# Adding x1 into the residual rows by an accumulating DMA instead of by identity products on TensorE

## The reference

```
x  = x + block(layernorm(x))                     # sublayer 1
     block(y): h  = layernorm(y, gamma, beta)
               h  = spiral_conv(h)               # long complex convolution over the 1024 tokens
               x1 = h + y
               return silu(layernorm(x1) @ w1 + b1) @ w2 + b2 + x1      # 128 -> 512 -> 128
x  = x + moe(layernorm(x))                       # sublayer 2
     moe(y):   the 2 best of 8 experts by y @ router, softmax over the two;
               each expert gelu(y @ w1[e] + b1[e]) @ w2[e] + b2[e]      # 128 -> 256 -> 128
```

## Time and profile before

| | us |
|---|---|
| three timed runs | 463.04, 464.27, 464.46 |
| their median | 464.27 |
| span of the profiled execution | 462.5 |
| TensorE busy in the span | 379.4 |
| VectorE busy | 357.4 |
| ScalarE busy | 321.8 |
| GpSimd busy | 268.1 |

### The profile page before, as it was taken

One profiled execution on the slowest core, in us unless ns is written; L12 is line 12 of the kernel. 1 busy time (PEld: TensorE's weight loads), 2 busy tenths in 40 slices (PEclk: granted clock), 3 DMA queues, 4 the chain that ended last, 5 costly groups with the idle time before them and its releaser, 6 DMA issues.

```text
span 462.5 us, 11382 instructions
## 1 busy us (share of the span) xinstructions
PE 379.4 (82%) x2812; PEld 339.3 (73%) x2812; DVE 357.4 (77%) x1329; ACT 321.8 (70%) x773; POOL 268.1 (58%) x331
## 2 busy tenths in 40 slices
PE   1274189989888889988897388999999999999980
PEld 1232168678676869686876388999999999999980
DVE  7999999978999999998176238777777777767770
ACT  4873387978887888867473536777777777777740
POOL 6980827452888888485627704676555555555551
PEclk9996569989999999999999569999999999999995
DMA  7649100000020202011203232444333333333200
GB/s 254 176 143 324 48 1 1 1 1 2 0 98 1 74 26 74 26 60 38 96 2 108 86 97 86 134 143 128 108 100 95 100 103 104 108 107 104 76 4 0
DMA packets 33283, 37.42 MB, mean 81 GB/s; under 512 B 5254, under 2 KB 29331, under 8 KB 33092
## 3 DMA queue, kind: packets, MB, share of 16 engines
q1 hardware_dynamic: 27236, 23.56, 18.0%
q0 software_dynamic: 5984, 13.13, 8.2%
HBM read 19.52 MB, written 18.92 MB: 83 GB/s over the span
## 4 chain that ended last, share of the span: by engine, by line
PE 56%; DVE 16%; ACT 9%; issue 5%; POOL 4%; POOLq 0%; DVEq 0%; ACTq 0%
PE up_p L999 12%; PE turn_p L999 6%; PE down_p L1018 6%; PE route_p L1018 6%; PE up_p L1018 5%; PE down_p L835 5%; PE turn_p L807 4%; DVE stats L1098 3%; ACT rows L655 3%; PE route_p L873 3%; ACT work L628 3%; PE down_p L1008 2%; DVE work L1162 2%; PE up_p L819 2%; DVE work L1160 1%
## 5 line engine op out<-in xcount | busy, mean ns | idle before, releaser
L590 POOL DMA_INDIRECT out<-result,out_id x91 | 89.2, 980 | 89.5 <-DVE result L1484 63.8
L556 POOL DMA_INDIRECT sorted_rows<-rows,pos x64 | 77.0, 1203 | 35.7 <-DVE pos L1217 18.4
L999 PE MATMUL up_p<-xt,work 128*128 128x128 f32 x488 | 66.5, 280 | 0.0
L781 ACT ACTIVATE work<-mw_c 128x256 f32 x182 | 65.5, 414 | 0.3 <-issue 0.2
L835 PEld LDWEIGHTS down_p<-w_sb,work 128*128 128x128 f32 x512 | 60.3, 192 | 4.9 <-issue 4.8
L835 PE MATMUL down_p<-w_sb,work 128*128 128x128 f32 x512 | 63.1, 277 | 0.0
L999 PEld LDWEIGHTS up_p<-xt,work 128*128 128x128 f32 x488 | 61.0, 196 | 0.2
L766 ACT ACTIVATE hid_t<-up_p 128x512 f32<-128x512 f32 x61 | 36.4, 597 | 30.3 <-PE up_p L999 29.7
L807 PE MATMUL turn_p<-ident,work 128*128 128x128 f32 x192 | 28.6, 298 | 28.4 <-ACT work L641 10.9
L615 ACT ACTIVATE work<-up_p,b_all 128x512 f32<-128x512 f32 x64 | 41.5, 680 | 14.3 <-PE up_p L821 14.2
L807 PEld LDWEIGHTS turn_p<-ident,work 128*128 128x128 f32 x192 | 24.0, 154 | 34.4 <-ACT work L641 11.6
(11 more groups left out here) (244 smaller groups left out, 896.5 us busy)
## 6 DMA issues: line engine op xcount, KB each, us to landing
tin<-sorted_rows SPq DMA_DIRECT2D x91, 136.0 KB, 2.1
resid<-in_x SPq DMA_DIRECT2D x8, 512.0 KB, 3.8
sorted_rows<-zeros SPq DMA_DIRECT2D x29, 136.0 KB, 2.3
out<-result,out_id POOLq DMA_INDIRECT x91, 2.2
work<-in_mw SPq DMA_DIRECT2D x1, 1024.0 KB, 6.2
sorted_rows<-rows,pos POOLq DMA_INDIRECT x64, 2.5
work<-in_w SPq DMA_DIRECT2D x1, 256.0 KB
w_sb<-in_w SPq DMA_DIRECT2D x1, 256.0 KB
```

The lines of the kernel that those rows point to most:

```text
L556: g.indirect_dma_start(sorted_dram, bass.IndirectOffsetOnAxis(pos[b % 2][:, j:j + 1], 0), rows[b % ROWBUFS][:, j, :], None).then_inc(s_sor ...
L590: g.indirect_dma_start(out_rows, bass.IndirectOffsetOnAxis(out_id[k][:, :], 0), result[k][:, :], None, bounds_check=TOKENS - 1, oob_is_err ...
L781: last = s_.activation(ring[s % RING][:, k * EF:(k + 1) * EF], mw1_c[:, bass.ds(at[k], EF)], ACT.Copy)
L999: last = t.matmul(mid_p[s % DEEP][:, c * TILE:(c + 1) * TILE], ring[s % RING][:, c * 128:(c + 1) * 128], xt[s % DEEP][:, :], start=True, s ...
```

## The change

The two identity products of `mlp_down(b, 0)` are removed, for each of the eight batches. In their place GpSimd issues one DMA per batch, `add_x1(b)`, which reads `x1[b % 2]` and adds it into the batch's rows of `resid`, both in SBUF, 128 partitions of 4096 bytes (512 KB). It is issued once `x1_sum(b)` is done and the last readers of the plain x rows of the batch (the two norms on ScalarE) are through. `x2_sum(b)` gets one more wait, on that DMA's own semaphore, before it reads `resid`.

```diff
--- before.py
+++ after.py
@@ -298,6 +298,7 @@
         s_up = sem("up_done")
         s_silu = sem("silu_done")
         s_dn = sem("down_done")
+        s_res = [sem(f"x1_in_residual{b}") for b in range(BATCHES)]
         s_x2 = sem("x2_ready")
 
         s_x2m = sem("x2_moments")
@@ -538,6 +539,13 @@
                 then(g.tensor_tensor(scale1[:, :], tmp[:, 1, :], neg_half[:, 0:TPB], ALU.pow))
                 g.tensor_tensor(shift1[:, :], tmp[:, 0, :], scale1[:, :], ALU.mult).then_inc(s_sc1, 1)
 
+            def add_x1(b):
+
+                pool.wait_ge(s_x1, b + 1)
+                pool.wait_ge(s_hn, b + 1)
+                pool.wait_ge(s_xn, b + 1)
+                g.dma_start(batch_of(resid, b), x1[b % 2], accum_op=ALU.add).then_inc(s_res[b], 16)
+
             def x2_scales(b):
                 pool.wait_ge(s_x2m, b + 1)
                 after(pool, s_xm, b)
@@ -563,6 +571,8 @@
                     x1_scales(b1)
                 if live(b0):
                     x2_scales(b0)
+                if live(b1):
+                    add_x1(b1)
                 if live(b3):
                     x0_scales(b3)
                 if live(chosen_b):
@@ -574,6 +584,7 @@
             sort_constants()
             x1_scales(0)
             x0_scales(2)
+            add_x1(0)
             for i in range(LAST):
                 iteration(i)
 
@@ -827,9 +838,6 @@
                     for h in range(2):
                         t.matmul(half(down_p, h), ones[:, :], b2_hi_lo[:, :], start=True, stop=False,
                                  skip_group_check=True)
-                    for h in range(2):
-                        t.matmul(half(down_p, h), ident[:, :], x1[b % 2][:, h * TPB // 2:(h + 1) * TPB // 2, :],
-                                 start=False, stop=False, skip_group_check=True)
                 pe.wait_ge(s_silu, b * 2 * FC + 2 * c + 2)
                 for j in range(TPB):
                     last = t.matmul(down_p[:, j * D:(j + 1) * D], silu[c % 2][:, j * TILE:(j + 1) * TILE],
@@ -1110,6 +1118,7 @@
 
             def x2_sum(b):
                 v.wait_ge(s_dn, (b + 1) * FC)
+                v.wait_ge(s_res[b], 16)
                 if live(b - ROWBUFS):
                     v.wait_ge(s_sort[b - ROWBUFS], 16 * TPB)
                 d.tensor_tensor(x2_of(b), tiled(down_p[:, :]), batch_of(resid, b), ALU.add).then_inc(s_x2, 1)
```

## The result

The changed kernel takes **466.04 us** (median of 7 runs, 465.79 to 467.58) against 464.41 us of the kernel before on the same chip (7 runs): a ratio of 1.0038, 95% interval 1.0021 to 1.0055, 1.6 us more. Two later measurements gave 1.0051 (1.0032 to 1.0071) and 1.0045 (1.0029 to 1.0061).

What follows compares the result with a forecast made beforehand. It took VectorE to bound iterations 2 and 3 and a VectorE-GpSimd-ScalarE-TensorE loop iterations 4 to 6. Span 462.5 - 0.5 + 2.4 + 0.2 + 0.3 = 464.9 us, given as median 466.6 us, range 462.9 to 472.0.

Steps and rivals of the forecast that it cites:

- So 1.26 us is covered: GpSimd: each DMA issue costs 1.26 us, hidden in waits of 1.8 us in iteration 2, 5.75 in iteration 5.
- Rival 2: GpSimd becomes the bound: issue exceeds the 1.8 us of room in iterations 2 to 4; 468.3 us at 3.3 us; chance 0.12.
- The rule of the Trainium skill that I weighed: GpSimd: VectorE blocks it only in two-port modes, so writing DMA descriptors should not suffer; issue 1.26 us anywhere.
- What the wider gaps do to TensorE's clock: TensorE: waits before place grow to 2.6 to 3.6 us, clock falls to half; 2.4 + 0.2 + 0.3 us, bounds 0 to 9.2.
- 0.8 us into each of iterations 4 to 6: TensorE: the part of a clock fall left on the path there, 0.8 us three times, 2.4 us.
- the case that I had bounded by 2.1 us: TensorE in iterations 4 to 6: a low-clock stretch lasting twice as long leaves 2.1 us on the path.
- covered by the same ScalarE norm, and its gain ends there: First batch: removing its identity product gains nothing, because ScalarE's norm covers it.
- Iteration 1, given 0.3 us: TensorE in iteration 1: the low-clock stretch already there may last longer, costing 0.3 us.
- Together the gain is 0.5 us of 15.3: TensorE: of 15.3 us of removed products only 0.4 us in iteration 1 and 0.1 in the tail shorten the path.
- TensorE's busy time lower by 15 us, unless the clock is low for longer: Sign on the changed profile: no identity product, TensorE busy some 15 us less unless its clock stays low longer.
- No wait of `x2_sum` on the DMA: VectorE's x2_sum: transfer of 7.6 us, at most 15, fits at least 23 us of room; the wait costs nothing.
- Iterations 2 and 3 keep VectorE's 25.4 us: Sign on the changed profile: these iterations, bound by VectorE, should keep their 25.4 us.

Runs made afterwards that it cites:

- experiment on iteration 4 alone: Changed kernel with identity products kept and the DMA moved behind x0_scales in iteration 4 only, in front elsewhere; 464.88 us, 0.9993.
- With GpSimd in time: Changed kernel with the DMA moved behind x0_scales: products gone 466.5 us, 1.0046; identity products put back 464.1 us, 0.9996.
- filler: Changed kernel plus four products of the identity with zeros in front of place in iterations 2 to 6; 468.11 us, 1.0085, and again 467.89 us, 1.0067.
- kernel with filler in iteration 0 as well: Changed kernel, DMA behind x0_scales, zero products before place in iterations 2 to 6 and in iteration 0; 463.85 us, 0.9976; without those in iteration 0, 1.0018.
- third session's profile: Profile of the unaltered changed kernel, run again beside the repeated filler run; 466.7 us, 1.0045.
- only the DMA: Changed kernel with its identity products put back, DMA in its first place, so x1 enters the sum twice; 466.86 us, 1.0061.

## Why the prediction was right, and where it was right by luck

The time (466.6 predicted, 466.04 measured), the direction and the range held. That the number is so close is luck: one cost was left out, and the cost that was counted was put too high in the iterations for which it was worked out. The steps:

**"So 1.26 us is covered"** is the step that failed. The price of an issue was right (0.99 us and 0.3), the room was not. I read the room in iteration 2 (1.8 us) and in iteration 5 (5.75 us) and took the iterations between for one or the other. The binding place is iteration 4, the last with `x0_scales`: before, the scatters waited 0.79 us there for `pos` and `x1_scales` 0.87 us for VectorE, 1.66 us together, and the push was more than the 1.26 us, because the small instructions behind the DMA slid under VectorE's products. In iteration 2 of the changed kernel the same rows took 0.2 to 0.5 us, and 1.55 us of waiting were left. Rival 2, at 0.12, therefore came true in a mild form, in one iteration and not three, 1.7 us late where I had priced 1.5. The experiment on iteration 4 alone shows it. The DMA with the products kept costs 1.0061, 2.8 us, a term that my sum puts at nothing.

The rule of the Trainium skill that I weighed (SBUF — State Buffer, Who interferes with whom) held for what I applied it to: the DMA's issue took 1.00 us beside a scan. The 3.01 us that I set against it was the row of an indirect DMA. My summary of the section was too short. The same section also says that a VectorE instruction with two inputs in SBUF contends with a GpSimd instruction that reads SBUF. The trace agrees (1.49 us beside 0.21 for the same instruction), and it is that sentence which applied to the instructions behind the DMA.

**"What the wider gaps do to TensorE's clock"**: the mechanism was right. The waits before `place` were 2.3 to 2.6 us and 3.4 us in iteration 6 (predicted 2.6 to 2.8 and 3.6), and falls followed some of them, not all. The size is open between 0.9 and 2.3 us, and the division was wrong. With GpSimd in time, products gone against products kept is 1.0046 against 0.9996, 0.5% or 2.3 us, where the forecast was 2.9 - 0.5 = 2.4 us. But with no DMA at all the products gone cost 1.0019 (1.0000 to 1.0038), 0.9 us, and that interval leaves 2.4 us out.

I had put 0.8 us into each of iterations 4 to 6. Where the clock fell behind `place` and the low stretch was as long as the recorded one, it cost 0 to 0.3 us (read where GpSimd was in time), so the waits behind covered nearly all of it. Only where it lasted twice as long, the case that I had bounded by 2.1 us, did it cost 1.0 to 1.6 us: in iteration 6 in four profiles, in iteration 4 in one.

I also gave iteration 0 nothing, "covered by the same ScalarE norm, and its gain ends there": I had asked only whether it could gain. In three of the nine profiles without product or filler there the clock was low from 76 to 79 us, and those three have the first start at 83.0 or 83.1, 1.3 us late. Iteration 1, given 0.3 us, takes 26.3 us in two profiles with a low stretch of 6.8 us, 0.7 more than before.

The kernel with filler in iteration 0 as well stands at 0.9976 against 1.0018, 1.9 us. That is more than a fall in a third of the executions would cost on the mean (an estimate: 1.3 / 3 = 0.4 us), the two were run on different chips, and neither profile has the fall at 76 us; what gives the rest is not shown.

**"Together the gain is 0.5 us of 15.3"**: right in size. Iteration 1 without a fall took 24.1 and 24.2 us with the product and 23.4 to 23.6 without, 0.6 us less (predicted 0.4); the tail is 19.5 us in both, nothing (0.1).

**The two costs don't add.** GpSimd's 3.0 us and the clock's 2.3 us would make 469.7; the changed kernel has 466.0 to 466.9. My sum had only one of them, so it hit. The DMA alone, with the products kept, has 466.9 us, as much as the changed kernel, so the measured time alone doesn't tell my mechanism from a late GpSimd. Each hides the other in two ways that the traces show: a fall behind `place` is spent in the wait for the late rows (iteration 5 of 25.67 us, above); and in the third session's profile a fall in iteration 4 (25.77 us) delayed `x1_sum` by so much that `x1_scales(6)` was in time.

**TensorE's busy time lower by 15 us, unless the clock is low for longer**: the second half applied, 7.1 us. **No wait of `x2_sum` on the DMA**: held, landing took 4.6 to 5.3 us. **Iterations 2 and 3 keep VectorE's 25.4 us**: held in all fourteen profiles.

Open is why the filler alone, twice, came out above "only the DMA" (1.0085 and 1.0067 against 1.0061, intervals that overlap), why the clock falls behind one wait and not behind an equal one, and with it how much of the 1 us won by the last kernel is the 0.6 us of iteration 1 and how much is another pattern of falls: all its 12 runs lie within 0.9 us, those of the kernel before within 3.

## What to carry to other kernels

Work taken from an engine that is off the path can buy nothing and can cost (here 0.9 to 2.3 us): it lengthens waits, and behind a longer wait TensorE's clock may be at half. Look first at which waits grow. The price of an instruction put into a full queue is not its own time but what the ones behind it meet when they run later, so read the room at every turn of the loop, and put the new one behind the small ones that something waits for. And two costs that end at the same wait are not summed; undo each with the other still in and with it out.

## What the runs showed of the hardware

- An accumulating DMA of 512 KB from SBUF to SBUF took 0.91 to 1.13 us on GpSimd and 4.6 / 4.7 / 5.3 us (min, median, max) to landing, and 1.00 us on GpSimd beside a VectorE scan; an indirect DMA with 128 rows took 2.8 to 3.0 us beside scans.
- GpSimd instructions on 8 or 16 elements per partition ended within 0.06 us of VectorE's product or scan that ran beside them: 1.49, 1.08 and 2.30 us in place of 0.21, 0.42 and 0.22.
- The granted clock fell after waits of TensorE of 1.8 to 3.4 us in some executions, and not after waits of 2.92 and 3.34 us in iteration 1 of others. In the tail of three filler profiles it fell behind waits of 0.94 to 0.96 and 0.62 us.
- Filler in front of one wait moved the fall behind the next one, and with it its price in iteration 5 from nothing to 1.7 us.
